# Attention tail of a four-batch block: the first query group projected ahead of the keys, and every root of the row norms on VectorE

## What is computed

```python
x = x + gat(ctx, layernorm(x))
h = rmsnorm(layernorm(x), attn_norm_w)
q, k, v = h @ q_w.T, h @ k_w.T, h @ v_w.T          # 16, 4 and 4 heads of 128
q, k = rope(rmsnorm(q, q_norm_w)), rope(rmsnorm(k, k_norm_w))
attn = softmax(causal(q @ k.T / sqrt(128))) @ v     # 4 query heads share one key head
hidden = layernorm(x) + attn @ o_w.T
x = x + hidden + moe(rmsnorm(hidden, ffn_norm_w))   # 8 experts, top 2, all computed
```

## Time and profile before

| | |
|---|---|
| median of 3 runs | 657.68 us (654.96 to 664.92) |
| profiled execution, its own time | 656.72 us |
| its span from first to last instruction | 654.9 us |
| mean granted TensorE clock | 0.979 of full |
| busy: TensorE / VectorE / ScalarE / GpSimd | 93% / 66% / 41% / 47% of the span |
| tail of batch 0 begins (first projection) | 126.08 us |
| tails of batches 1, 2, 3 begin | 274.86, 422.99 us and some 115 us later |

### The profile page before, as it was taken

How to read it: one execution, slowest core, us unless ns; L and a number is a source line. 1 busy time by engine, 2 the same in 40 slices (tenths; PEclk the granted TensorE clock), 3 DMA queues, 4 the chain that set the end, 5 groups by cost and what they waited for, 6 DMA issues and landing times.

```text
span 654.9 us, 10357 instructions
## 1 busy us (share of the span) xinstructions
PE 607.1 (93%) x3269; PEld 435.6 (67%) x3269; DVE 435.1 (66%) x1279; ACT 269.0 (41%) x653; POOL 306.8 (47%) x588
## 2 busy tenths in 40 slices
PE   3799899789799999989699999989999998999998
PEld 2278468336677798736587788736668873666886
DVE  4897688598755587599756487466644646664463
ACT  2363454164665342164665342045740204574020
POOL 1493486478844240378854150378630038763000
PEclk9999899889899999999899999989999998999999
DMA  8920000000000000000000000000000000000000
GB/s 285 385 72 3 1 2 1 16 5 2 1 1 2 1 2 17 16 2 1 1 2 1 1 2 0 18 0 2 1 1 1 2 17 1 2 0 2 1 2 16
DMA packets 8729, 14.41 MB, mean 22 GB/s; under 512 B 908, under 2 KB 7372, under 8 KB 8420
## 3 DMA queue, kind: packets, MB, share of 16 engines
q1 hardware_dynamic: 8676, 13.76, 5.9%
HBM read 12.70 MB, written 1.05 MB: 21 GB/s over the span
## 4 chain that ended last, share of the span: by engine, by line
PE 65%; DVE 19%; issue 5%; POOL 5%; ACT 4%; DMA 1%; DVEq 0%; POOLq 0%; SPq 0%; ACTq 0%
PE bank L616 14%; PE bank L514 10%; PE bank L574 5%; PE ob L488 5%; PE bank L638 5%; PE bank L593 4%; PE bank L560 3%; PE tb L477 3%; DVE ssq L1024 2%; PE bank L589 2%; PE bank L585 2%; ACT prob L727 2%; DVE tt L959 2%; DVE m L1021 2%; PE zb L469 2%
## 5 line engine op out<-in xcount | busy, mean ns | idle before, releaser
L560 PE MATMUL bank<-wqkv_sb,hT 128*128 128x512 f32 x192 | 92.8, 623 | 0.8 <-ACT v_sb L703 0.8
L727 ACT ACTIVATE prob<-bank,sneg,rms 128x128 f32<-128x128 f32 (+1 forms) x128 | 64.0, 508 | 58.6 <-DVE sneg L1053 58.4
L837 POOL TENSOR_TENSOR m<-early,rope_s 128x256 f32<-128x256 f32 x80 | 73.1, 938 | 31.4 <-ACT early L708 30.9
L514 PE MATMUL bank<-m,wgu_sb 128*128 128x128 f32 (+1 forms) x480 | 85.6, 329 | 0.7 <-DVE early L1100 0.6
L795 POOL TENSOR_SCALAR tt<-tt,gmn 128x256 f32<-128x256 f32 x96 | 66.9, 706 | 36.2 <-DVE gmn L959 35.8
L514 PEld LDWEIGHTS bank<-m,wgu_sb 128*128 128x128 f32 x480 | 70.9, 191 | 8.9 <-DVE early L1100 2.1
L853 POOL TENSOR_SCALAR prob<-prob,srcp 128x128 f32<-128x128 f32 (+1 forms) x128 | 53.4, 435 | 48.2 <-DVE srcp L1124 48.0
L574 PE MATMUL bank<-kT,qT 128*128 128x128 f32 (+1 forms) x256 | 60.9, 354 | 1.8 <-ACT prob L727 1.8
L616 PE MATMUL bank<-wo_sb,qT 128*128 128x256 f32 x256 | 59.0, 382 | 0.7 <-ACT qT L733 0.7
L560 PEld LDWEIGHTS bank<-wqkv_sb,hT 128*128 128x128 f32 x192 | 35.4, 196 | 36.3 <-issue 33.0
L708 ACT ACTIVATE early<-bank 128x512 f32<-128x512 f32 x40 | 24.1, 602 | 79.5 <-PE bank L560 77.2
(11 more groups left out here) (200 smaller groups left out, 1182.3 us busy)
## 6 DMA issues: line engine op xcount, KB each, us to landing
wqkv_sb<-wqkv_dram SPq DMA_DIRECT2D x1, 3072.0 KB, 12.2
wgu_sb<-wgu_dram SPq DMA_DIRECT2D x2, 1408.0 KB, 10.8
wo_sb<-wo_dram SPq DMA_DIRECT2D x1, 2048.0 KB, 17.6
wd_sb<-wd_dram SPq DMA_DIRECT2D x1, 1408.0 KB, 14.7
out_dram<-rows SPq DMA_DIRECT2D x8, 128.0 KB, 1.7
xin<-x_dram SPq DMA_DIRECT2D x3, 256.0 KB, 2.7
rows<-gat_rows_dram SPq DMA_DIRECT2D x2, 256.0 KB, 2.9
kT<-x_dram SPq DMA_DIRECT2D x1, 256.0 KB, 3.8
```

Source lines behind the costliest of these rows:

```text
L514: mm = pe.matmul(ps[:, m * N + c0:m * N + c1], wgu_sb[:, m, k, n * P:(n + 1) * P], tokT[:, k, c0:c1], start=(k == 0), stop=(k == KT - 1))
L560: mm = pe.matmul(ps[:, :], hT[:, k, t * P:(t + 1) * P], wqkv_sb[:, k, c * G * HD:(c + 1) * G * HD], start=(k == 0), stop=(k == KT - 1))
L727: ins = act.activation(prob[:, n % 5, i * nk:(i + 1) * nk], ps[:, i * nk:(i + 1) * nk], ACT.Exp, bias=sneg[:, n, i:i + 1], scale=rq(g, t, ...
L837: ins = pool.tensor_tensor(dst[:, :, c, :], src[:, :, 1 - c, :], s_, ALU.mult)
```

## The change

`QKV_AT` stays, but the projections now come as query group 0 (t=0, t=1), keys (t=0, t=1), values, then the other three query groups. Blocks 0 and 1 are that query group, blocks 2 and 3 the keys; `LOGICAL` maps a block to the old numbering. The two query transposes come at steps 5 and 6, ahead of the keys' transposes at steps 8 and 9. The keys' sum stands at projection 4 (step 5) and their product with the root at projection 5 (step 6), where both stood at step 4. A key transpose now waits for its own half alone.

The Newton steps of all three root groups go to VectorE in every batch (`ROOTS_ON_VECTOR`), in a form of three instructions each, right behind the first guess. So do those of the prep, for `LN2_AT`.

```diff
+ROOTS_ON_VECTOR = (0, 1, 2, 3)
...
-TURN_AT = (6, 7, 8, 9, 10, 11, 11, 12, 13, 14)
+TURN_AT = (5, 6, 8, 9, 10, 11, 11, 12, 13, 14)
+LOGICAL = (2, 3, 0, 1, 4, 5, 6, 7, 8, 9)
+KEYS = (2, 3)
...
-                    if n < T:
-                        pe.wait_ge(k_ready, (b + 1) * T)
+                    if n in KEYS:
+                        pe.wait_ge(k_ready, b * T + KEYS.index(n) + 1)
...
                 if a == LN2_AT[1]:
-                    pool.wait_ge(ln_seed, b + 1)
+                    pool.wait_ge(ln_ready, b + 1)
                     pool.nop(nofuse=True)
-                    for _ in range(3):
-                        newton(link_a, b, ln_y[:, :], ln_a[:, :], ln_v[:, :])
-                    pool.sem_inc(ln_ready, 1)
...
                     first_guess(link_a, b, ln_y[:, :], ln_a[:, :], ln_v[:, :])
-                    dve.sem_inc(ln_seed, 1)
+                    for _ in range(3):
+                        newton(link_a, b, ln_y[:, :], ln_a[:, :], ln_v[:, :])
+                    dve.sem_inc(ln_ready, 1)
                 if a == LN2_AT[2]:
-                    dve.wait_ge(ln_ready, b + 1)
-                    dve.nop(nofuse=True)
...
-                    if u in (1, 5, 9):
+                    if u in (3, 5, 9):
...
-                        dve.tensor_scalar(y.bitcast(I32), a.bitcast(I32), -1, MAGIC, ALU.mult, ALU.add).then_inc(seed_ready, 1)
-                elif kind == "qkv" and n == 3:
-                    dve.wait_ge(m2_ready, b * QU + 5)
-                    dve.wait_ge(m1_ready, b * QU + 5)
-                    for u in range(T):
+                        ins = dve.tensor_scalar(y.bitcast(I32), a.bitcast(I32), -1, MAGIC, ALU.mult, ALU.add)
+                        if b not in ROOTS_ON_VECTOR:
+                            ins.then_inc(seed_ready, 1)
+                        else:
+                            link_b(b, ins)
+                            for _ in range(3):
+                                newton(link_b, b, y, a, v)
+                            if u > 3:
+                                dve.tensor_scalar(y, y, SCALE, None, ALU.mult).then_inc(rms_ready, 1)
+                            else:
+                                dve.sem_inc(rms_ready, 1)
+                elif kind == "qkv" and n == 4:
+                    dve.wait_ge(m2_ready, b * QU + 7)
+                    dve.wait_ge(m1_ready, b * QU + 7)
+                    for u in KEYS:
                         ins = dve.tensor_tensor(m1[:, u, :], m1[:, u, :], m2[:, u, :], ALU.add)
-                    link_b(b, ins)
+                    keys_at[0] = mark_b(ins)
+                elif kind == "qkv" and n == 5:
+                    dve.wait_ge(dve_b, keys_at[0])
                     dve.wait_ge(rms_ready, b * 3 + 1)
```

More of the change, by code:

```diff
@@ L122, with block_of, rows_of @@
 assert MIXT_AT[0] > UPDOWN_AT[6]
+def block_of(n):
+    return n if n < 4 else n - T
+def rows_of(u):
+    m = LOGICAL[u]
+    return (1, 0, m) if m < T else (0, *divmod(m - T, T))
 def work(s):
@@ L557, in fill @@
                 if kind == "qkv":
-                    c, t = (HKV, n) if n < 2 else (HKV + 1, n - 2) if n < 4 else divmod(n - 4, 2)
+                    if n in (4, 5):
+                        c, t = HKV + 1, n - 4
+                    else:
+                        key, g, t = rows_of(block_of(n))
+                        c = HKV if key else g
                     for k in range(KT):
@@ L711, in empty @@
                     filled(act, b, w)
-                    if n < 2:
-                        dst = kT[:, :, n * P:(n + 1) * P]
+                    key, g, t = rows_of(n)
+                    if key:
+                        dst = kT[:, :, t * P:(t + 1) * P]
                     else:
-                        g, t = divmod(n - 2, 2)
                         dst = qT[:, G * g:G * g + G, t * P:(t + 1) * P]
@@ L756, in _ @@
         def _(pool):
-            links, links_a = [0], [0]
+            links = [0]
             def link(b, ins):
@@ L815, in inverse_rms @@
                 v, y, a = ssq[:, lo:hi], rms[:, lo:hi], rms_a[:, lo:hi]
-                pool.wait_ge(seed_ready, b * 3 + c + 1)
+                pool.wait_ge(seed_ready, (b - len([v for v in ROOTS_ON_VECTOR if v < b])) * 3 + c + 1)
                 for _ in range(3):
@@ L826, in part @@
                 kind, n = w
-                if kind == "qkv" and n not in (2, 3):
-                    u = n if n < 2 else n - 2
-                    which, t = (1, u) if u < 2 else (0, u % 2)
+                if kind == "qkv" and n not in (4, 5):
+                    u = block_of(n)
+                    which, _, t = rows_of(u)
                     pool.wait_ge(raw_ready, b * QU + u + 1)
@@ L838, in part @@
                     ins.then_inc(m2_ready, 1)
-                    if u in (1, 5, 9):
-                        inverse_rms(b, (u - 1) // 4)
+                    if u in (3, 5, 9) and b not in ROOTS_ON_VECTOR:
+                        inverse_rms(b, (3, 5, 9).index(u))
                 elif kind == "oproj":
@@ L872, in _ @@
             count = [0, 0]
-            mixed = [0]
+            mixed, keys_at = [0], [0]
             def link_a(b, ins):
@@ L1023, in part @@
                     emptied(dve, b, w)
-                    ins = dve.tensor_reduce(ssq[:, u * G:(u + 1) * G], sq[:, u % 3, :].rearrange("p (h d) -> p h d", h=G), AX.X, ALU.add)
+                    ins = dve.tensor_reduce(ssq[:, LOGICAL[u] * G:(LOGICAL[u] + 1) * G], sq[:, u % 3, :].rearrange("p (h d) -> p h d", h=G), AX.X, ALU.add)
                     ins.then_inc(m1_ready, 1)
-                    if u in (1, 5, 9):
-                        lo, hi = ((0, 2 * G), (2 * G, 6 * G), (6 * G, 10 * G))[(u - 1) // 4]
+                    if u in (3, 5, 9):
+                        lo, hi = ((0, 2 * G), (2 * G, 6 * G), (6 * G, 10 * G))[(3, 5, 9).index(u)]
                         v, y, a = ssq[:, lo:hi], rms[:, lo:hi], rms_a[:, lo:hi]
@@ L1253, in _ @@
                     reciprocals(b, s)
-            assert count[1] == B * N_B, count
+            assert count[1] == B * N_B + 30 * len(ROOTS_ON_VECTOR), count
 def kernel(**inputs):
```

20 lines of the change are left out of this document (9 added, 11 removed).

## The result

The changed kernel took 672.32 us (median of 4 executions, 671.23 to 676.47) against 656.32 us of the kernel before on the same chip (median of 4, 654.85 to 664.92): a ratio of 1.0242 with a 95% interval of 1.0169 to 1.0315. It is slower; whether by more than 2%, the interval does not tell. The profiled execution has a span of 671.6 us, 16.7 more than the 654.9 before.

A forecast was written before the change was run, and what follows sets the result against it. VectorE was taken to set the pace in batches 0 and 1, waiting for GpSimd's key root in 2 and 3. 0.9 + 1.7 + 11.2 - 2.4 + 3.4 = 14.8 on 656.72 gave 671.5 us, range 660 to 680.

The forecast's parts named there:

- Preps: Preps' roots on VectorE: 0.9 us later in batch 0 and 0.55 us in each of three others, 2.6 us in all.
- First `sneg` of batches 0 and 1: Heads of batches 0 and 1: two root groups on VectorE delay the first `sneg` by 3.4 us, between 2.5 and 5.3.
- Third group: Batches 0 and 1, ahead of score 1's row maximum: 2.2 us more per batch, wait at L477 growing to 3.4 us.
- Without the roots GpSimd's large work falls beside rounds that were quick: VectorE ahead of the first `sneg`, batches 0 and 1: GpSimd's large work slows its rounds, 0.5 us net, between 0 and 2.3.
- Clock: TensorE behind grown waits, L477 in batches 0 and 1, the score in 2 and 3: low clock costs 3.4 us, 0 to 6.8.
- two of the four: Of four waits growing to about 3 us, two were counted as bringing a low-clock stretch, 3.4 us together.
- Batches 2 and 3: Key wait gone, about 1.2 us of gain left per batch at score 3, where the wait becomes some 3 us: -2.4 us.
- The first `sneg` (451.06) comes 3.3 to 4 us earlier, since both its root and the transposes do: Batch 2: root on VectorE and earlier query transposes bring the first `sneg` 3.3 to 4 us forward.
- 0.9 for `hn`: Prep of batch 0: root on VectorE adds 1.75 us less the 0.83 us `hn` waited for GpSimd, so 0.9 us later.
- TensorE does not set the pace in batches 0 and 1: Denies the rival that TensorE sets the pace everywhere, roots fit VectorE's room and key waits go: 643.3 us, chance 0.08.
- The two kinds of batch cancel: Rival: VectorE's lengthening at its lower end (9.4 us), no clock lost, batches 2 and 3 gain 8.8: 660 us, chance 0.22.
- The roots themselves are stretched: Rival: GpSimd stretches half of each group's nine root instructions on VectorE, 2.2 us more a group: 680 us, chance 0.10.

The follow-up runs named there:

- prep_gpsimd: The changed kernel with only the Newton steps of the preps moved back to GpSimd: 671.41 us, ratio 1.015 to 1.026 to the kernel before.
- changed_filled_wide: The changed kernel with unread matmuls in TensorE's waits in batches 0 and 1, 44 ahead of L586 and 34 ahead of L491: 668.67 us.
- third_gpsimd: The changed kernel with only the third root group of batches 0 and 1 back on GpSimd: 667.66 us, ratio 1.013 to 1.017 to the kernel before.
- changed_filled_twice: The changed kernel with unread matmuls in TensorE's waits in batches 0 and 1, 44 ahead of L586 and 18 ahead of L491: 669.09 us.

## Why the prediction was right, and where not

The time, the sign and the range held: 671.5 us (660 to 680) against 672.32. Its terms one by one, from the profiled executions:

- **Preps**, 2.6 us: right in the waits, 0.92 + 3 x 0.54 = 2.5; the median of prep_gpsimd is too wide to show it.
- **First `sneg` of batches 0 and 1**, 3.4 us: right, 3.35. By the runs 0.9 of it is the order and 2.45 the roots; the prediction had put it all on the roots, so that the size came out by luck. The lower bound of 2.5 is not its own sum, which gives 3.95 - 1.0 = 2.95.
- **Third group**, 2.2 us: right as a price (2.09), mis-sized as a term, since net it is 1.1 and the wait at L491 2.37 us instead of 3.4. The step that failed is "Without the roots GpSimd's large work falls beside rounds that were quick": I counted GpSimd's freedom as a loss of 0.5 ahead of the first `sneg` and as nothing behind it, and there it is a gain of 0.98.
- **Clock**, 3.4 us as "two of the four" stretches of 1.7: mis-sized. Behind L491 it came in both batches, lasted 7 us and not 3.4, and cost 3.0 each, 6.0 together, which keeping the clock up gave back in the profile. In batch 1 of prep_gpsimd it lasted 3.4 us behind a like wait and cost 1.7, as priced (4.61 us from third to fourth `sneg` instead of 2.94). In batches 2 and 3 the stretch moved from the key wait to a later place: in batch 2 behind score 3, in batch 3 behind L586, where the wait at score 3 shrinks from 2.76 to 1.09 us. Behind score 3 it is the dearer: batch 2 has 116.66 us with it there, and 115.79 in changed_filled_wide, whose clock fell behind L586.
- **Batches 2 and 3**, -2.4 us: failed. The key wait did go and the wait at score 3 of batch 2 came as forecast (2.76 against "some 3 us"; 1.09 in batch 3). The step that failed is "The first `sneg` (451.06) comes 3.3 to 4 us earlier, since both its root and the transposes do": it came 1.9 us earlier, by the order alone, and with the roots on VectorE 0.08 later than without. The key's root did come 1.6 us sooner. But I had forgotten that the second group also stands ahead of that `sneg`, 4.95 us long and in series with two blocks, which takes the 1.6 back. The third group's 2.2 us ahead of the second `sneg` was right (2.16). Together +1.4 in place of -2.4, without the preps.
- **Not in the sum**: the lead-in was shorter by 1.6 us in spite of its 0.9 for `hn`. Behind the same wait of 2.07 us before batch 0 the clock fell in the kernel before and not in the changed one. No part of the change explains it. The wait, and the windows behind it:

```profile
77.74 0.57 PE L469 MATMUL zb<-pair_r,pair_l 48*128 48x512 bf16 x1 [2.07 <-ACT zs L686]
...
77.17 0.37 PE L483 MATMUL zb<-pair_r,pair_l 48*128 48x512 bf16 x1 [2.07 <-ACT zs L704]
```

```profile
78.00:84.00 6.00, 6.00 (x15) 1.47 (x14) 5.43 (x18) 2.17 (x4) 4.37 (x5) 0.50 0.01 3
...
78.00:84.00 6.00, 6.00 (x28) 2.30 (x26) 5.90 (x21) 3.01 (x7) 5.38 (x5) 1.00 0.00 0
```

Of each pair the first row is of the kernel before, the second of the changed one. The other runs say that this is the luck of one execution: seven of them have the changed kernel's lead-in, the clock fell there in all seven, and their batch 0 begins at 125.79 to 126.88 us. In the mean it begins at 126.1 us in the eight profiles with this lead-in and at 125.3 in the six with the old one, which is in line with the forecast's 0.9.

So the sum came out by errors that cancel: 2.2 too much for the third groups and 2.5 that the lead-in gave, against 2.6 too little for the clock and 3.8 for batches 2 and 3. That 671.5 lies so near is luck. Sound are the sign, and the two terms that lengthen VectorE in batches 0 and 1, with 4.5 us per batch in place of 5.6.

The rivals: TensorE does not set the pace in batches 0 and 1, since the first `sneg` moved with VectorE. "The two kinds of batch cancel" fell at its own point, the wait at score 3 of batch 2; its first condition held (VectorE's lengthening is 3.35 + 1.11 us a batch, 8.9 for two, against its 9.4), the clock and batches 2 and 3 did not follow it. "The roots themselves are stretched" is partly true: the nine Newton rows of the second and third group of batches 0 and 1 ran at 0.17 to 0.18, but the second group of batch 2 was stretched by 2.4 us, 0.9 of it on two Newton rows and the rest on the first guess. It does not carry the result, since batches 2 and 3 together lost only 2 us. The rule of the Trainium skill cited with it holds for two-input instructions and for those in a 2-port mode. All three root instructions are of the first kind and not two of them, since L908 takes the same tensor twice; the rows show one-input ones stretched as well (L1039 to L1041), whose mode no run shows.

What stays open: why the same wait is followed by a low clock in one batch or execution and not in another, and why the clock fell twice in the middle of a tail (third_gpsimd, changed_filled_twice), where TensorE had had no wait of 0.25 us or more for over 60 us. The runs show what it costs, and that at L491 a wait filled nearly whole kept the clock up behind it; they do not show what decides. Nor do they show why the order alone brings the first `sneg` of batches 0 and 1 0.9 us later.
